# Down product in seven block products, with the sums of h made in stage one and stored by GpSimd's queue

## The reference

```python
gate = x @ Wg + (x @ Ag[a]) @ Bg[a]          # Wg, Wu: 512 x 2048; rank 16, 8 adapters
up   = x @ Wu + (x @ Au[a]) @ Bu[a]
h    = silu(gate) * up
x    = x + h @ Wd + (h @ Ad[a]) @ Bd[a]      # Wd: 2048 x 512
x    = x + einsum('bct,bcd->bdt', x, w1[a])  # a = itok_B_0_7, one adapter per sequence
```

## Time and profile before

| | us |
|---|---|
| median of 3 runs | 1229.32 (1228.62 to 1229.39) |
| profiled execution, device time | 1230.07 |
| its span, first to last instruction | 1228.4 |
| PE busy | 1197.1 (97%) |
| DVE busy | 758.4 (62%) |
| ACT busy | 517.1 (42%) |
| POOL busy | 119.7 (10%) |
| mean granted clock of TensorE | 0.991 |

### The profile page before, as it was taken

How to read it: one execution, slowest core, us unless ns; L and a number is a source line. 1 busy time by engine, 2 the same in 40 slices (tenths; PEclk the granted TensorE clock), 3 DMA queues, 4 the chain that set the end, 5 groups by cost and what they waited for, 6 DMA issues and landing times.

```text
span 1228.4 us, 22972 instructions
## 1 busy us (share of the span) xinstructions
PE 1197.1 (97%) x7104; PEld 1072.3 (87%) x7104; DVE 758.4 (62%) x1338; ACT 517.1 (42%) x983; POOL 119.7 (10%) x207
## 2 busy tenths in 40 slices
PE   4899999999999999999999999999999999999997
PEld 3678888888888888888888888899999999999997
DVE  6666667766676766667766677654554544554543
ACT  4544444544444544444544454443333333333332
POOL 5223100001100000100000000011111111111110
PEclk8899999999999999999999999999999999999999
DMA  5597664776566578557466777666545555545530
GB/s 191 165 279 234 207 177 128 196 226 193 157 187 172 144 199 244 152 161 197 122 193 195 215 212 214 187 198 197 156 144 161 164 173 153 157 144 167 172 106 36
DMA packets 113629, 217.15 MB, mean 177 GB/s; under 512 B 26338, under 2 KB 68450, under 8 KB 113506
## 3 DMA queue, kind: packets, MB, share of 16 engines
q1 hardware_dynamic: 104096, 190.41, 53.6%
q0 software_dynamic: 8544, 23.60, 5.8%
q10 hardware_dynamic: 866, 1.66, 0.4%
HBM read 169.43 MB, written 46.14 MB: 175 GB/s over the span
## 4 chain that ended last, share of the span: by engine, by line
PE 46%; SPq 2%; issue 1%; DVE 1%; DMA 1%; ACT 1%; ACTq 0%
PE ps L1138 6%; PE ps L1142 5%; PE ps L1146 5%; PE ps L1145 5%; PE ps L1140 5%; PE ps L1147 4%; PE ps L991 4%; PE ps L992 4%; PE ps L993 4%; PE ps L1003 2%; SPq L270 1%; PE ps L1173 1%; PE ps L1174 1%; PE ps L1175 1%; SPq L165 1%
## 5 line engine op out<-in xcount | busy, mean ns | idle before, releaser
L991 PE MATMUL ps<-xo_hi,w_hi 128*128 128x512 f32 x896 | 357.1, 398 | 11.2 <-DVE w_lo L684 10.5
L992 PE MATMUL ps<-xo_lo,w_hi 128*128 128x512 f32 x896 | 352.9, 394 | 0.0
L993 PE MATMUL ps<-xo_hi,w_lo 128*128 128x512 f32 x896 | 350.3, 391 | 0.0
L991 PEld LDWEIGHTS ps<-xo_hi,w_hi 128*128 128x128 f32 x896 | 170.1, 190 | 41.2 <-DVE w_lo L684 10.5
L993 PEld LDWEIGHTS ps<-xo_hi,w_lo 128*128 128x128 f32 x896 | 169.1, 189 | 37.5
L992 PEld LDWEIGHTS ps<-xo_lo,w_hi 128*128 128x128 f32 x896 | 170.2, 190 | 26.3
L1003 PEld LDWEIGHTS ps<-t_st,bq 128*128 128x128 f32 x1024 | 157.5, 191 | 28.8 <-POOL bq L345 6.6
L684 DVE TENSOR_TENSOR hl<-h_raw,hh 128x1024 fp32r<-128x1024 f32 x64 | 78.4, 1225 | 154.6 <-ACT hh L417 154.6
L1003 PE MATMUL ps<-t_st,bq 128*128 128x256 f32 x1024 | 164.4, 284 | 7.7 <-POOL bq L345 5.8
L1138 PE MATMUL ps<-wd_hl,hh 128*128 128x320 f32 x512 | 160.2, 313 | 0.0
L684 DVE TENSOR_TENSOR w_lo<-wsum,w_hi 128x512 fp32r<-128x512 f32 x116 | 82.2, 708 | 123.7 <-ACT w_hi L417 123.7
(11 more groups left out here) (76 smaller groups left out, 1546.0 us busy)
## 6 DMA issues: line engine op xcount, KB each, us to landing
bq<-b_dram SPq DMA_DIRECT2D x992, 64.0 KB, 2.2
h_dram<-h_f SPq DMA_DIRECT2D x64, 512.0 KB, 3.6
h_raw<-h_dram SPq DMA_DIRECT2D x64, 512.0 KB, 4.1
raw<-packed SPq DMA_DIRECT2D x58, 512.0 KB, 5.3
ad_raw<-a_d SPq DMA_DIRECT2D x64, 128.0 KB, 2.8
xs<-x POOLq DMA_DIRECT2D x16, 512.0 KB, 5.2
y_out_dram<-ys POOLq DMA_DIRECT2D x30, 256.0 KB, 3.5
xst<-xg SPq DMA_DIRECT2D x14, 512.0 KB, 6.4
```

Source lines behind the costliest of these rows:

```text
L991: pe.matmul(bank, st[0], mv[0], start=start and kk == 0, stop=False, skip_group_check=True)
L992: pe.matmul(bank, st[0], mv[1], start=False, stop=False, skip_group_check=True)
L993: m = pe.matmul(bank, st[1], mv[0], start=False, stop=kk == 1, skip_group_check=True)
```

## The change

**Stage two** computes the down product as a 2 x 2 block product too: tokens in two tiles of 128, hidden features by even and odd chunk (8 chunks each, `KC`), outputs in two halves of 256 (`HD`). Seven products per pair (H11, HS1, H22, HS2, H12, HS3, HS4), each of 8 chunks of three matmuls: 288 columns where the product carries the adapter's columns (WD11, WDT1, WDN4, WD21), 256 elsewhere. A pair now takes one tile from each half of a group of 1024 tokens (`seq_of`). Partial products are added to the residual tile one by one (`add_p1`, `add_p5`, `add_u2`, `add_p4`, `add_u3`, `make_x11`, `make_x12`, `make_x22`, 256 elements each). The turns and low-rank products of a pair now lie inside the same pair; only the mixing lies in the next one (in HS1, for pair 1 in HS2).

**The sums of h** (HS1 to HS4) are made by DVE in stage one, per two steps, in three tiles `hs1` to `hs3`, and stored by GpSimd's queue; the program of that queue now goes step by step. The plain blocks of h are stored by SP (`store_even`, `store_odd`), now ahead of the gathers of the step. h_dram is laid out by pair and product: every block of a step and group is 256 KB in rows of 128 tokens, 512 B; seven blocks per two steps where there were two of 512 KB. `load_h` reads 512 KB per product, seven per pair instead of four.

**The sums of Wd** (T1, T3, T2, N4) are made by DVE in steps 51 to 58 in pieces of 512 elements; T3 and N4 go to DRAM and come back to where they are needed. T1 and W11 are split in steps 59 to 62; T2 and N4 (whole planes of 2048 elements) in step 63, W21, T3 and W22 in pair 0. The order in which they are split is `WD_ORDER`.

**Tables.** B_d and w1 are split once for all adapters (`table_hi`, `table_lo`, around step 34) and stored to DRAM; stage two gathers the finished rows (4 transfers for B_d instead of 12, 8 for w1 instead of 4) and splits nothing there. In group 0 the making of t for the next group comes five steps later (`LATE_T`). The adapter's register loads of the next group are spread over eight steps. The fifth of the seven x residues moves from the last step of a group to the first of the next.

```diff
+LATE_T = 5
...
+H11, HS1, H22, HS2, H12, HS3, HS4 = range(PRODUCTS)
+WD11, WDT1, WDN4, WDT2, WD21, WDT3, WD22 = range(PRODUCTS)
+WD_ORDER = (WDT1, WD11, WDT2, WDN4, WD21, WDT3, WD22)
+AD_SLOTS = (WD11, WDT1, WDN4, WD21)
+AD_SLOT_AFTER = ((4, 5, 6, 6), (1, 2, 4, 5))
...
+            def store_op(s, op, tile, col):
+                g, k = s // CH, chunk_of(s) // 2
+                sp.dma_start(h_dram[PPG * g:PPG * (g + 1), op, :, k, :].rearrange("q p t -> p q t"),
+                             tile[:, col:col + HALF].rearrange("p (q t) -> p q t", q=PPG)).then_inc(h_stored[op], 16)
+
+            def store_even(s):
                 sp.wait_ge(h1_done, s + 1)
+                store_op(s, H11, h_f[0], 0)
+
+            def store_odd(s):
                 sp.wait_ge(h2_done, s + 1)
-                sp.dma_start(h_dram[4 * g:4 * g + 4, :, c, :].rearrange("q p t -> p q t"),
-                             h_f[s % 2][:, :].rearrange("p (q t) -> p q t", q=4)).then_inc(h_stored[s % 2], 16)
+                store_op(s, H22, h_f[1], HALF)
+                sp.wait_ge(h1_done, s + 1)
+                store_op(s, H12, h_f[1], 0)
...
+            def load_n4():
+                sp.wait_ge(wdn4_stored, 16)
+                sp.wait_ge(w_lo_done, 3 * (load_no(STEPS - 1) + 1))
+                sp.wait_ge(p4_done, STEPS - 1)
+                load_parts(WDN4, WLO, wd_dram[1])
...
+                if s % 2:
+                    store_even(s - 1)
+                else:
+                    store_odd(s - 1)
...
+            load_n4()
+            load_h(1)
+            load_wd21()
+            load_h(2)
+            load_h(3)
+            load_wdt3()
+            load_h(4)
+            load_bd(0)
+            load_h(5)
+            load_wd22()
+            load_h(6)
+            store_odd(STEPS - 1)
+            load_ad(1)
+            for n in range(3, PAIRS * PRODUCTS):
+                p, i = divmod(n, PRODUCTS)
+                if n + 4 < PAIRS * PRODUCTS:
                     load_h(n + 4)
+                if i == 3 and p + 1 < PAIRS:
+                    load_bd(p + 1)
+                if i == 5 and p + 2 < PAIRS:
+                    load_ad(p + 2)
...
+            def store_sum(s, op, tile, col):
+                g, k = s // CH, chunk_of(s) // 2
+                pool.dma_start(h_dram[PPG * g:PPG * (g + 1), op, :, k, :].rearrange("q p t -> p q t"),
+                               tile[:, col:col + HALF].rearrange("p (q t) -> p q t", q=PPG)).then_inc(h_stored[op], 16)
+
+            def store_s3(n):
+                pool.wait_ge(hs3_done, n + 1)
+                store_sum(2 * n, HS3, hs3, 0)
+
+            def store_s12(n):
+                pool.wait_ge(hs1_done, n + 1)
+                store_sum(2 * n, HS1, hs1, 0)
+                pool.wait_ge(hs2_done, n + 1)
+                store_sum(2 * n, HS2, hs2, 0)
+
+            def store_s4(n):
+                pool.wait_ge(hs4_done, n + 1)
+                store_sum(2 * n, HS4, hs2, 0)
...
+            for s in range(1, STEPS):
+                g, c = divmod(s, CH)
+                late = LATE_T if g == 0 else 0
+                if s < PIECES:
+                    b_lo(s)
+                    store_b(s)
+                    if s + 1 < PIECES:
+                        load_b(s + 1)
+                if g + 1 < GROUPS and 4 <= c - late < 8:
+                    gather_a(g + 1, c - late - 4)
+                if s == 2 * CH:
+                    load_tables()
+                if s == 2 * CH + 3:
+                    store_tables()
+                if s % 2:
+                    store_s3(s // 2)
+                    if s >= 3:
+                        store_s4(s // 2 - 1)
+                else:
+                    store_s12(s // 2 - 1)
...
+            def wd_hi(op):
+                lo_at = WLO if op in AD_SLOTS else HD
+                if op == WDT1:
+                    act.wait_ge(t1_done, 4)
+                    act.wait_ge(wdt3_stored, 32)
+                elif op == WDT2:
+                    act.wait_ge(t2_done, 4)
+                    act.wait_ge(p5_done, STEPS)
+                else:
+                    act.wait_ge(wd_in[op], 16 * len(wd_raw[op]))
+                if op == WD11:
+                    act.wait_ge(wdn4_stored, 16)
+                for w, r in zip(wd_hl[op], wd_raw[op]):
+                    m = hi(w[:, :, 0:HD], wd_y[:, :, :] if op == WDT2 else r[:, :, lo_at:lo_at + HD])
+                m.then_inc(wd_hi_done, 1)
...
+            def make_s3(n):
+                dve.wait_ge(h1_done, 2 * n + 1)
+                dve.wait_ge(h2_done, 2 * n + 1)
+                if n:
+                    dve.wait_ge(h_stored[HS3], 16 * n)
+                dve.tensor_tensor(hs3[:, :], h_f[0][:, 0:HALF], h_f[0][:, HALF:GT], ALU.subtract).then_inc(hs3_done, 1)
+
+            def make_s1(n):
+                dve.wait_ge(h2_done, 2 * n + 2)
+                if n:
+                    dve.wait_ge(h_stored[HS1], 16 * n)
+                dve.tensor_tensor(hs1[:, :], h_f[0][:, HALF:GT], h_f[1][:, HALF:GT], ALU.add).then_inc(hs1_done, 1)
+
+            def make_s2(n):
+                dve.wait_ge(hs1_done, n + 1)
+                if n:
+                    dve.wait_ge(h_stored[HS4], 16 * n)
+                dve.tensor_tensor(hs2[:, :], hs1[:, :], h_f[0][:, 0:HALF], ALU.subtract).then_inc(hs2_done, 1)
+
+            def make_s4(n):
+                dve.wait_ge(hs2_done, n + 1)
+                dve.wait_ge(h1_done, 2 * n + 2)
+                dve.wait_ge(h_stored[HS2], 16 * (n + 1))
+                dve.tensor_tensor(hs2[:, :], h_f[1][:, 0:HALF], hs2[:, :], ALU.subtract).then_inc(hs4_done, 1)
...
+                if s % 2 == 0:
+                    make_s1(s // 2 - 1)
+                    make_s2(s // 2 - 1)
+                elif not last:
+                    make_s3(s // 2)
+                    if s >= 3:
+                        make_s4(s // 2 - 1)
...
+            def down(n, k, start):
+                p, i = divmod(n, PRODUCTS)
+                ra, rb, rc, rd = banks(p)
+                bank = {H11: ra, HS1: rc, H22: rd, HS2: ra, H12: rb, HS3: ra, HS4: rc}[i]
+                w = wd_chunk(i, k)
+                width = HD + TR if i in AD_SLOTS else HD
+                h_hi, h_lo = hh[n % 3][:, k, :], hl[n % 3][:, k, :]
+                pe.matmul(bank[:, 0:width], h_hi, w[:, 0:width], start=start and k == 0, stop=False, skip_group_check=True)
+                pe.matmul(bank[:, 0:width], h_hi, w[:, width:2 * width], start=False, stop=False, skip_group_check=True)
+                return pe.matmul(bank[:, 0:width], h_lo, w[:, 0:width], start=False, stop=False, skip_group_check=True)
...
+                pe.wait_ge(h_lo_done, n + 1)
+                if p == 0:
+                    pe.wait_ge(wd_lo_done, WD_ORDER.index(i) + 1)
+                if i in AD_SLOTS:
+                    pe.wait_ge(ad_lo_done, 4 * p + AD_SLOTS.index(i) + 1)
+                if i == HS2:
+                    pe.wait_ge(p1_added, p + 1)
+                if i == HS3:
+                    pe.wait_ge(u2_added, p + 1)
+                if i == HS4:
+                    pe.wait_ge(p5_added, p + 1)
+                for k in range(KC):
+                    m = down(n, k, i in (H11, HS1, H22, H12))
+                    if k == KC - 1:
+                        m.then_inc(product_done, 1)
+                    at = i, k
+                    if p and at == ((HS2, 5) if p == 1 else (HS1, 1)):
+                        mix_tile(p - 1, 0)
+                    if p and at == ((HS2, 6) if p == 1 else (HS1, 5)):
+                        mix_tile(p - 1, 1)
+                    if at == ((H12, 2) if p else (HS3, 5)):
+                        turn(p, 1)
+                    if at == ((HS3, 1) if p else (HS4, 1)):
+                        lora_down(p, 1, 0, rd).then_inc(lora_21_done, 1)
+                    if at == (HS4, 2 if p else 3):
+                        turn(p, 0)
+                    if at == (HS4, 6):
+                        lora_down(p, 0, 0, rb).then_inc(lora_11_done, 1)
+                        lora_down(p, 0, 1, rc)
+                        pe.wait_ge(u3_added, p + 1)
+                        lora_down(p, 1, 1, ra).then_inc(lora_22_done, 1)
```

More of the change, by code:

```diff
@@ L219, in gather_b @@
                 g, k = divmod(n, PIECES)
-                if k == first == 0:
-                    for b in range(SLOTS):
-                        slot_numbers[b] = number(sp, g * SLOTS + b)
                 sp.wait_ge(b_stored, 16 * (k if g == 0 else PIECES))
@@ L625, in _ @@
                     b_hi(s)
-                if 5 <= c < 9 and g + 1 < GROUPS:
-                    t_hi(g + 1, c - 5)
+                late = LATE_T if g == 0 else 0
+                if 5 <= c - late < 9 and g + 1 < GROUPS:
+                    t_hi(g + 1, c - late - 5)
+                if s == 2 * CH + 2:
+                    table_hi()
                 silu_1(s)
@@ L782, in make_h1 @@
             def make_h1(s):
+                if s >= 2:
```

(13 more changed lines are left out.)

961 lines of the change are left out of this document (563 added, 398 removed).

## The result

The changed kernel takes 1216.4 us (median, 1215.33 to 1219.65), the kernel before 1229.32: ratio 0.9901, 95% interval 0.988 to 0.9921. That is 12.9 us faster where 36 were forecast. The profiled execution took 1219.65 us, its span is 1218.0, the mean granted clock 0.982 (0.991 before).

A forecast was written before the change was run, and what follows sets the result against it. Both stages were taken as paced by PE's matmul stream. 1230.1 - 46 (stream) + 1 (slips) + 8 (entry) - 1.7 (end) + 2 (stage one) = 1193.4, taken as 1193 us; range 1180 to 1218.

The forecast's parts named there:

- The stream of stage two: PE's matmuls in stage two: 2.9 us less a pair, 46 us in 16 pairs, a steady pair 23.3 us.
- rival A: Stage two: hand-offs pace it, a pair loses 1 us or more, 1209 at 1 us a pair; chance 0.20.
- Stage one, queues: Stage one: SyncE's queue, tied to h, would still issue gathers in time; GpSimd's added stores and waits would cost nothing.
- 3 us of room: Stage one: gathers of a piece's second half land 3 us before PE wants them, against 5 in the kernel before.
- +2: Stage one: cost of 2 us with DMA engines below full, as Wd moves hold back gathers; bounds 0 and +10.
- rival C: Stage one: SyncE's queue late with gathers, PE waits a microsecond every two steps, +32, 1225 us; chance 0.08.
- The small rows: Stage one: seven stores of h per two steps in 512-B rows raise the DMA share from 0.62 to 0.85.
- Rival B: Stage one: 512-B rows at the price of 1-KB rows fill the DMA engines, +57, 1250 us; chance 0.10.
- The entry: Last step of stage one and pairs 0 and 1: PE waits 9 us instead of 1.0, +8; bounds +1 and +16.
- The end: After the last product: the remaining chain lasts 7.8 us against 9.5, -1.7, between -3 and 0.
- a first down matmul after 810 us: Start of stage two, expected at 800 to 803 us: later than 810 would mean late gathers or full DMA engines.
- DVE waiting for h_stored in the steps: Stage one: DVE waiting on stores of h in the steps would show the forecast wrong; no size given.

The follow-up runs named there:

- the kernel before with it: Kernel before, with its store of h ahead of the loop's gathers and register loads spread over eight steps: 1234.74 us, ratio 1.0049.
- the three orders: Changed kernel with x loads one step later, load_ad(2) one place later in pair 0, and gathers ahead of the stores of h: 1196.71 us, ratio 0.9739.
- T3 earlier: Changed kernel with late x loads and late load_ad(2), plus plane T3 of Wd split before td_hi and td_add in pair 0: 1205.07 us, ratio 0.9812.

## Why the prediction was right and wrong

**The stream of stage two: right.** Forecast 23.3 us a pair, measured 23.40 in each steady pair, and hand-offs don't pace it (rival A falls): from 850 to 1200 us PE is busy 345.86 of 350. DVE is at 246.50 / 350 = 70%, not 79%: the price of a residue of h held (1.22 us), but the durations of neighbouring instructions overlap, as the 1.22 us from 851.43 and the start of the next at 852.56 below show. Over the ten pairs from 932 to 1166 us DVE's durations sum to 183 us, 78% of the time, and cover only 166, 71%. The 49% that the forecast set beside its 79% was such a covered share, so the two could not be compared. The DMA share is 0.71 where 0.83 was forecast, though the bytes are as forecast (242 GB/s x 23.4 us = 5.7 MB a pair). 16 x 2.8 leave the term at -45.

**Stage one, queues: this step failed.** "3 us of room" for the second half of a piece, and with it the term "+2", at most +10, was wrong: measured +22.5. 14.0 us are more waiting for gathers; about 6.5 are the price of the half clock, since PE worked 12.9 us of it in three intervals (3.4, 10.2 and 3.4 us, the second begun while PE still stood); the rest are tenths in many steps, most of them in group 0. The mechanism is that of rival C, and the forecast's reasoning against it had three gaps. First, the room was worked out for a mean pair of steps: gathers, stores, at most two weight loads. It left out the x loads, which stand in the program between the two halves of a piece. In the kernel before they stood there too, but in the later groups SP had a lead over the steps; tied to h it has none, and with them and a slower first half the issue came 3.9 us into step 36, where 2.8 us ahead of it had been forecast. Second, it took 2.3 us from issue to landing. Behind the x loads it was 3.8 to 7.2 us even in the kernel before, and 6.1 to 9.2 in the changed one; at steps 4 and 20 this alone used up the room. It also took 7.53 us for sixteen issues from one row: of the sixty such groups in stage one of the kernel before, that is all but the shortest (7.51 to 10.77, median 7.95), and the changed kernel has 7.52 to 12.94, median 8.3, so that the issue is not slower in general, but in some places. Third, a wait was priced at its length, while the rows at 484 and 488 show that the half clock behind it costs again. Rival C's own price, 1 us every two steps, was wrong in shape: the lateness isn't even, it comes in lumps of 2 to 10 us where another load stands ahead. That the tie costs something alone is shown by the kernel before with it: 5.4 us.

**The small rows: cheaper than every bound.** The forecast took a share of 0.85, between 0.76 and 1.08; measured is 0.71 in stage one. Two things were wrong. The 65 ns of a 1-KB row were read in a burst in which the engines were full; the mean over 200 to 600 us of the same kernel is 55. And four of the seven stores are GpSimd's, whose rows cost 19 ns each, since they travel in 4-KB packets. In SyncE's stores 512 B cost 28 ns, 0.51 of 1 KB. Rival B, which needed 0.88 of the 1-KB price, is refuted. (Its other mark, the gain used up at 0.97, comes out at 0.96 from the forecast's own terms.) The Trainium skill (DMA: Bandwidth & Descriptors, Why small descriptors are slow), with its fixed cycles per packet, led to an estimate of 0.54 for this ratio, which the traces bear out, and of 0.78 for the share, which they put too high for the two reasons above. The volume acted through the lumps: some 11 us of the median with the x loads between the halves, 3.6 with them behind. At step 36, where it acted most, 2.9 us were earlier issue and 1.2 earlier landing; for the rest of the 11 us the two were not separated.

**The entry: right in kind, too small in size.** Forecast +8, measured about +13.3: 387.5 = 419.2 - 45 + 13.3. The waits for residues of h (6.0), for the added U2 (1.7) and for td_t (1.3) sum to 9.0. That this is the sum forecast is luck, for its parts are others: the wait for U3 of the last step (0.4) did not come, before the product with W22 PE stood 0.6 us instead of 1.3, for a reason that the profile doesn't show, the wait before HS1 was 2.2 instead of 1.7, the one before HS3 1.7 instead of 2.6, and for U2 instead of T3, the one for the turned sums 1.3 instead of 1.9, and the one in pair 1 3.77 instead of 1. There the forecast had seen the h load behind load_ad(2), but not that load_ad(2) itself waits for a buffer until the adapter residues of pair 1 are made. DVE makes the last of them at 854.23, behind two of the last sums of h (1.4 us), and SP issues at 855.43:

```profile
851.43 1.22 DVE L886 TENSOR_TENSOR hl<-h_raw,hh 128x1024 fp32r<-128x1024 f32 x1
852.56 0.69 DVE L1007 TENSOR_TENSOR hs<-h_f,h_f 128x512 f32<-128x512 f32 x1
853.28 0.69 DVE L1013 TENSOR_TENSOR hs<-hs,h_f 128x512 f32<-128x512 f32 x1
```

Another 3.4 us are the clock: 3.4 us at 0.50, twice, from the waits at about 828 and 866 on, where the forecast had only said that this lies within its bound of +16. With the 0.6 and less the 1.0 us waited before, 12 of the 13.3 us are accounted for.

**The end: right**, 8.3 us for 7.8 expected. The operations on whole planes of 2048 elements, which no row had shown, were priced at 2.3 and 1.9 us and took 2.29 on DVE and 1.92 on ACT.

**Signs.** The prediction named a first down matmul after 810 us as the sign for B or C; it is 822.2, and the waits for gathers name C. Another of its signs, DVE waiting for h_stored in the steps, came too, twice in group 0 (1.8 us at step 3 and 2.7 at step 4). With the three orders stage one ends at 801.6, the +2 forecast, and the time is 1196.7 against 1193: the rest of the sum holds, up to the entry. The time lies inside the range, at its upper end of 1218, because A and the bounds had widened it, not because C was weighed rightly; that is luck.

**Open.** With the three orders 4.2 us of waiting for the added U2 stay in the entry, with the DMA engines full (1.05) from 804 to 824; whether the order on ACT and DVE or the loads set them was not settled, and the one attempt (T3 earlier) moved nothing.

## What to carry to other kernels

When a store is put ahead of loads on one in-order queue, the queue loses its lead over the whole program: list every instruction of it, the rare ones too (x loads once in 16 steps, register loads once a group), at the real time at which each would then be issued, and look for the one that falls ahead of a transfer with a deadline. What stands ahead costs twice, in the issue and in the landing: take the landing time of such a transfer from the place where it is slowest (7.2 us before, at step 4), not a median. A mean per period says nothing of these. Price a stall of PE with the half clock that follows, and after a change that adds volume try the order of the queue before cutting the volume: here three moved places gave 20 us, and three quarters of the sums' bytes after that only 3.6.

## What the hardware showed

- In stores from SBUF to DRAM a packet of 512 B takes 28 ns of one DMA engine in the mean and one of 1 KB 55 ns (SyncE's stores of h in the changed kernel and the kernel before, 200 to 600 us); the 65 ns from the earlier trace rows were read while the engines were full.
- The queue that issues decides the packets: GpSimd's rows of 512 B went in packets of 4.1 KB (13.0 MB in 3164 packets), 19 ns a row, SyncE's one by one.
- Gathers of 64 KB land 2.6 us after their issue in the median, but in the changed kernel the last one behind 2 MB of x loads only after 6.1 to 9.2 us; with the x loads moved behind them, after 2.2 to 4.6 us.
- SP's issue of sixteen gathers isn't constant: 7.51 to 10.77 us in the kernel before, 7.52 to 12.94 in the changed one. The longest group lay beside five stores by GpSimd; with these a step earlier the group in its place took 8.46 us.
- 16 register loads in a block hold SP for 9.7 us, some 0.6 us each.
- GpSimd's queue takes 0.75 us per store of a sum (128 stores, 96.0 us), in rows of 512 B, and 0.54 us when it stores a quarter of the rows.
- A stand of PE can bring the granted clock down to 0.50, but not each does: in the changed kernel's stage one it fell with the stands of 4.2, 7.2 and 2.2 us, for 3.4, 10.2 and 3.4 us, and not with one of 1.7 us; in the kernel before with the store ahead, a stand of 2.9 us at step 4 left it at 1.00.
